# Second mixture's gating inside the second attention by groups of batches, and its two passes with hidden units on partitions

## What is computed

```python
gate_weights = softmax(einsum('bld,de->ble', x, gate_W) + gate_b)      # 8 experts
topk_vals, topk_idx = top_k(gate_weights, 2)
boost = x
for i in range(2):        # experts: relu(x W1[e] + b1[e]) W2[e] + b2[e], hidden 256
    eo = selected_expert(boost, topk_idx[:, :, i], W1, b1, W2, b2)
    outs.append(eo)
    if i < 1: boost = boost + 0.5 * eo
fused = sum(topk_vals[:, :, i:i + 1] * outs[i])
return layer_norm(x + fused, gamma, beta)    # and all of it takes layernorm(x) as its x
```

## Time and profile before

| What | us |
|---|---|
| Median of 3 runs (1680.38 to 1689.57) | 1687.01 |
| The profiled execution | 1688.53 |
| Its span, first to last instruction | 1686.7 |
| Second attention ends | 1390.2 |
| Gating, from there to the first pass's first load | 98.6 |
| First pass | 89.3 |
| Second pass, to the end of the span | 108.6 |

### The profile page before, as it was taken

One profiled execution on the slowest core, in us unless ns is written; L12 is line 12 of the kernel. 1 busy time (PEld: TensorE's weight loads), 2 busy tenths in 40 slices (PEclk: granted clock), 3 DMA queues, 4 the chain that ended last, 5 costly groups with the idle time before them and its releaser, 6 DMA issues. The chain is left out here.

```text
span 1686.7 us, 36701 instructions
## 1 busy us (share of the span) xinstructions
PE 1428.5 (85%) x12500; PEld 940.8 (56%) x12500; DVE 1094.9 (65%) x2690; ACT 858.2 (51%) x1437; POOL 684.8 (41%) x1037
## 2 busy tenths in 40 slices
PE   3799999999999979989999548999999985058583
PEld 1255555555555547669999514555566655046452
DVE  3778778788787726744444447888888745336483
ACT  1567677776766656314444214566666654023242
POOL 2223242332323111463333256566653214635287
PEclk8699999999999989999999867999999995579796
DMA  4111211212112003701212133333332202444341
GB/s 128 57 47 35 64 52 34 66 38 61 51 34 66 20 28 125 101 14 48 49 48 49 30 76 83 76 88 79 78 80 70 72 7 99 144 137 152 88 122 44
DMA packets 92373, 115.54 MB, mean 68 GB/s; under 512 B 13090, under 2 KB 75841, under 8 KB 91936
## 3 DMA queue, kind: packets, MB, share of 16 engines
q1 hardware_dynamic: 75360, 91.63, 19.7%
q0 software_dynamic: 16832, 21.56, 5.6%
HBM read 73.67 MB, written 39.21 MB: 67 GB/s over the span
## 5 line engine op out<-in xcount | busy, mean ns | idle before, releaser
L688 DVE TENSOR_REDUCE wm<-wsm 128x16 f32<-128x512 f32 x512 | 330.1, 685 | 112.7 <-PE wsm L428 109.7
L585 ACT ACTIVATE we<-wst 128x1024 f32<-128x1024 f32 x320 | 325.1, 1022 | 120.0 <-PE wst L461 109.0
L585 ACT ACTIVATE ce<-cst 128x896 f32<-128x896 f32 (+1 forms) x256 | 172.6, 704 | 136.2 <-PE cst L456 116.9
L684 DVE TENSOR_REDUCE cnm<-csm 128x1 f32<-128x512 f32 (+3 forms) x352 | 213.1, 636 | 42.9 <-PE csm L425 37.0
L428 PE MATMUL wsm<-wks,wqs 96*128 96x512 bf16 x512 | 173.4, 394 | 9.1 <-DVE wm L688 5.6
L461 PE MATMUL wst<-wqs,wks 128*128 128x512 bf16 x512 | 149.8, 384 | 0.3 <-ACT we L585 0.3
L1718 PE MATMUL abup<-abxt,abws 128*128 128x128 f32 x1120 | 138.7, 278 | 0.4 <-ACT abxt L1744 0.4
L421 PE MATMUL csm<-cks,cqs 96*128 96x256 bf16 (+3 forms) x512 | 131.5, 309 | 6.9 <-DVE cnm L684 5.0
L1718 PEld LDWEIGHTS abup<-abxt,abws 128*128 128x128 f32 x1120 | 132.6, 194 | 0.7 <-ACT abxt L1744 0.7
L495 PE MATMUL woa<-we,wv 128*32 128x128 f32 (+2 forms) x2560 | 130.6, 340 | 0.0
L814 POOL TENSOR_TENSOR wdif<-wglb,wloc 128x16 f32<-128x16 f32 x32 | 7.1, 221 | 290.2 <-DVE wloc L710 290.2
(11 more groups left out here) (327 smaller groups left out, 3037.1 us busy)
## 6 DMA issues: line engine op xcount, KB each, us to landing
wqs<-qk_parts SPq DMA_DIRECT2D x96, 96.0 KB
wks<-qk_parts SPq DMA_DIRECT2D x96, 96.0 KB
cqs<-qk_parts SPq DMA_DIRECT2D x96, 96.0 KB
cks<-qk_parts SPq DMA_DIRECT2D x96, 96.0 KB
b1r<-rows SPq DMA_DIRECT2D x40, 194.0 KB
qk_parts<-wpt SPq DMA_DIRECT2D x48, 128.0 KB
qk_parts<-cpt SPq DMA_DIRECT2D x48, 128.0 KB
b0r<-rows SPq DMA_DIRECT2D x40, 130.0 KB
```

What stands on the lines that cost most here:

```text
L585: act.activation(E[:, e_slot(g, i), 0:width], ST[:, (U * g + i) % 2, 0:width], ACT.Exp, scale=SCALE).then_inc(s_ex, 1)
L684: dve.tensor_reduce(NM[:, n % 2, first:first + heads, t], got, AX.X, ALU.max).then_inc(s_mx, 1)
L688: dve.tensor_reduce(M[:, n % 2, hs, t, :].rearrange("p (w f) -> p w f", f=DIL), SM[:, j % 2, :].rearrange("p (w i f) -> p w f i", w=NT, f= ...
```

## The change

The second mixture's tiles become an object `Gate` made before the attention. New events in the attention's list gate a finished batch while later batches run: normalise (`g_norm`, `g_rows`), turn and logits (`g_turn`, `g_logits`), and for groups of batches (0,1), (2,3), (4,5), (6), (7) softmax and choice (`g_soft`, four parts), count, places (`g_place`) and scatters. The gated rows lie in a ring of three batches. Running totals of a group (`BASE`) are the next group's bases. After the last slot stand the same events for batch 7, then `finish`: the padding of pass 0 by SP and of pass 1 by ACT, eight blocks each, and the first table; the second table is made by DVE in the first iterations of pass 0. The loads of weights are issued in batches 1, 2 and 7; W2 takes the place of tiles that the attention no longer needs.

In the passes ACT copies the expert's W1 to a fixed tile, which is then the stationary side: the hidden units lie on partitions, b1 is a bias by partition inside the relu, and no transpose of the hidden layer is needed. b2 enters by a product of ones with a tile that has b2 in its first row. All numbers of experts are read at a pass's start; 39 blocks are run. In the second pass ACT takes the root, DVE the reciprocal, the scale and the last addition.

```diff
+        def gating(b, g, at, put):
+            if g == 0 and b in (1, 2, B - 1):
+                put(4, "loads", {1: 0, 2: 1}.get(b, 2))
+            if g == 1:
+                put(3, "g_norm", b - 1)
+                put(6, "g_rows", b - 1)
+            if g == 2:
+                put(1, "g_turn", b - 1)
+                put(3, "g_logits", b - 1)
+            for q, (lo, hi) in enumerate(GROUPS):
+                if b == hi:
+                    if g == 2:
+                        put(4, "g_soft", q, 0)
+                        put(5, "g_soft", q, 1)
+                        put(7, "g_soft", q, 2)
+                    if g == 3:
+                        put(0, "g_soft", q, 3)
+                        put(1, "g_count", q)
+                        put(3, "g_place", q)
+                tiles = [(c, t) for c in range(lo, hi) for t in range(NT)]
+                if b == B - 1 == hi and g == 3:
+                    for c, t in tiles:
+                        put(6, "scatter", c, t)
+                elif b == hi + 1 and hi < B - 1:
+                    for c, t in tiles[2 * g:2 * g + 2]:
+                        put(2 + 3 * (t % 2), "scatter", c, t)
...
         order += [("evac", SLOTS - 1), ("sel", SLOTS - 1), ("heads_T", B - 1), ("out_proj", B - 1)]
+        if gate:
+            b, q = B - 1, len(GROUPS) - 1
+            order += [("g_norm", b), ("g_rows", b), ("g_turn", b), ("g_logits", b)]
+            order += [("g_soft", q, part) for part in range(4)] + [("g_count", q), ("g_place", q)]
+            order += [("scatter", b, t) for t in range(NT)] + [("finish", 0)]
...
+            def g_place(q, turn):
...
+                dve.tensor_copy(PO, counted(T)).then_inc(s_gc, 1)
+                dve.wait_ge(s_gc, q + 1)
+                if q:
+                    for b in range(*GROUPS[q - 1]):
+                        dve.wait_ge(s_sc[b % RING1], 16 * NT * (b // RING1 + 1))
+                bases = [const["base"] if q == 0 else gate.BASE[:, (q - 1) % 2, j, :] for j in range(2)]
+                route.place(st, dve, PO, 0, T, bases)
...
+            for i in range(N + 1):
                 if i + 1 < N:
                     turn_rows(i + 1)
+                if i < N:
...
+                        m = pe.matmul(UP[:, i % 2, c, 0:P], WS[:, i % 2, c * P:(c + 1) * P], XT[:, i % 2, :], start=True,
+                                      stop=True)
...
+                    pe.matmul(Y[:, j % 2, 0:D], const["ones"], B2[:, bass.ds(e * D, D)], start=True, stop=False)
+                    for c in range(HB):
+                        pe.wait_ge(s_h[c], j + 1)
+                        m = pe.matmul(Y[:, j % 2, 0:D], HT[:, j % 2, c, :], W2[:, bass.ds(e * HB * D + c * D, D)],
+                                      start=False, stop=(c == HB - 1))
...
+                    act.copy(WS[:, j % 2, :], W1[:, bass.ds(e * F, F)]).then_inc(s_ws, 1)
...
+                        act.activation(HT[:, i % 2, c, :], UP[:, i % 2, c, 0:P], ACT.Relu, bias=bias(known, i, c)
...
+                    act.activation(std[:, j % K:j % K + 1], mv[:, j % K, 1:2], ACT.Sqrt, bias=eps[:, :]).then_inc(s_sd, 1)
...
+                    dve.tensor_scalar(HT[:, i % 2, 0, :], UP[:, i % 2, 0, 0:P], bias(known, i, 0), 0.0, ALU.add, ALU.max
+                                      ).then_inc(s_h[0], 1)
```

1092 lines of the change are left out of this document (560 added, 532 removed).

## The result

| | kernel before | changed kernel |
|---|---|---|
| median of 20 runs, us | 1685.76 | 1681.22 |
| lowest to highest | 1680.38 to 1689.88 | 1671.97 to 1692.11 |
| ratio | | 0.997 (0.9956 to 0.9985) |
| profiled execution | 1688.53 | 1673.89 |

What follows compares the result with a forecast made beforehand. The prediction took the gating as an uncovered chain and POOL as setting the second pass's end; 1688.53 - 64.6 (gating) + 43 (attention) - 3 - 19 (passes) = 1644.9, forecast 1645 us, range 1612 to 1676.

Steps and rivals of the forecast that it cites:

- The attention's term: Second attention, with the gating moved under it: +43 us, bounded between 15 and 100.
- (a): Slot g1 of the attention: statistics, aggregates, token column and shift on DVE lengthen its windows, 13 us.
- (b): Logits behind `rows` in one bank: PE waits for ACT to empty it, then runs them; 1.9 x 7 = 13 us.
- (c): Groups' softmax, choice, places and counting in the attention, with the last slot's wait for scatters: together 14 us.
- The wait of DVE for scatters in the last slot: Attention's last slot: DVE waits at i3 for scatters POOL issues at i5, PE's last `sel` queued behind; 3.4 us.
- signs of being wrong: In the changed profile: a batch longer by 12 or more, DVE steps of 0.5 and more beside POOL, or ACT busiest in a pass.
- Rival 3: Attention: DVE's small steps stall behind POOL's instructions and stall PE; 1702, deciding from 0.43 us a step; chance 0.1.
- The gating's tail: Gating left after the attention, one batch's, ended by the padding: 34 us in place of 98.6, -64.6.
- The shift: DVE's step in the last batch's gating after the attention: 0.2 us.
- the padding: SP's 8 transfers at 1.56 us in the gating's tail, the later branch, with 2.1 behind to land.
- The passes: Two passes after the gating: 86.0 us (-3) and 89.5 us (-19), at 1.70 us a warm block.
- The sum of cases: Whole kernel: chances added over forecast and rivals, faster by more than about 0.5% 0.90, same 0.03, slower 0.07.

Runs made afterwards that it cites:

- b1_wait7: Kernel before, plus one PE wait behind `rows` in slot g2 of batches 1 to 7, until ACT has emptied the bank; 1683.6 us, ratio 1.003.
- b2_wait28: Kernel before, plus the PE wait behind `rows` in all 28 slots whose rows belong to batches 1 to 7; 1703.2 us, ratio 1.0142.
- c_after: The changed kernel without an edit, run again on chip 2; 1634.8 us, ratio 0.9755 to the kernel before.
- d1_fixed: Changed kernel, PE in the passes always taking expert 0's W2 and b2 and reading no table; 1678.6 us, ratio 0.994 to the kernel before.
- a2_lazy: Changed kernel, each engine in the passes reading a table word when first needed, not ten ahead; 1640.5 us, ratio 0.9776 to the kernel before.

## Why the prediction was wrong

**The attention's term failed, +43 for +70.8.** By its parts:
- (a), slot g1, forecast 13: the seven windows grew by 20.9, by 3.0 in batches 1, 2 and 4 and by 5.0 in batch 3. In batch 3 POOL's scatters for the first group fall into the same slot, beside its gathers for the first mixture; that this makes the 5.0 is not tested (batch 5 has scatters too, and grew by 3.3). In batch 1 DVE's work is 2.0 more than in the earlier trace rows (12.35 for 10.40), about as forecast, but its idle time grew by 1.0 too, and PE waited 1.0 for score maxima behind the burst.
- (b), the wait for the bank, 1.9 a batch: right where the clock held (1.8 in batch 3). The stall's own price is shown by b1_wait7 and b2_wait28, 0.7 to 0.9.
- (c), the groups, and (b) together: slots g2 and g3 were to grow by 30 (POOL's 3 among them) and grew by 48.3. In it are 22 for the clock, and without them 26. Within this, what I had not seen is that PE itself would stand at the count, 8.4 us in three places; I had priced the steps on DVE and forgotten who waits for their end. The wait of DVE for scatters in the last slot was 6.4, not 3.4, by the view of its waits:

```profile
DVE bAT L1371 <- DMA rows<-brows,bIDX: 6.4, 1, 6.4
```

- The step that failed is one that the working doesn't have. I read "granted 0.53" in the earlier trace rows as a property of the gating, and 1.00 in every window of the earlier trace rows as a given. PE's own products were priced at full clock, and waits at their length. That a stage at full clock can lose it when waits of 1 to 3 us are put in it was neither a term nor a rival; it is worth some 22 of the 28 us missing. The other 6 to 8 are waits of PE beyond those priced: idle time grew by 36, and 28 were forecast for it. c_after bears this out: with 27.2 us at half clock its attention is 61.9 longer than that of the kernel before (364.7 for 302.8), and less half of 27.2 this is 48, as 70.8 less 22 is 49. What exactly makes the clock fall at one place and not at its twin isn't settled by these runs.

Of the signs of being wrong that were named, one was met: a batch longer by 12 or more. The three windows of batches 2 and 4 grew by 12.4 each, where 8 was forecast, those of batches 1 and 3 by 8.1 and 6.9, where 4 was.

**Rival 3 fell, though the time lies in its range.** It was to come about by DVE steps of 0.43 us and up; the 1681 came about another way. DVE's routing steps in the attention beside POOL's work, the window of their line alone (busy time, count, then clock and DMA):

```profile
1085.00:1459.00 374.00, 30.41 (x129) 0.94 0.27 72
```

and one of the groups of that line (count, shortest, median and longest in ns):

```profile
L1371 DVE TENSOR_TENSOR bV<-bV,cgmx x8: 191/225/1054, 1159.7 to 1438.4; 128x64 f32<-128x64 f32 x6, 128x32 f32<-128x32 f32 x2
```

30.41 us in all, 0.236 each; four of the 129 took 1.05 to 1.12 beside an instruction of POOL (the 1054 above is one). The rule of the Trainium skill ("SBUF — State Buffer", section "SBUF: two separate sides") thus shows at single steps, and at the shift of the last batch, but does not decide the time.

**The gating's tail was right.** 35.9 for 34. The shift took 1.23 beside POOL's addition where I had taken 0.2, and the padding ended it, as forecast. Its two last parts were off in opposite ways: the padding took 10.2 for 12.5, and 6.9 passed from its end to the first load (1494.95) where 2.1 were taken. The timeline of the changed kernel:

```profile
1461.80 1.25 POOL L1129 TENSOR_TENSOR brows<-X,bbe 128x512 f32<-128x512 f32 x1
...
1461.85 1.23 DVE L624 SCALAR_TENSOR_TENSOR cgsh<-cgmv,cgrs 128x4 f32<-128x4 f32 x1 [1.36 <-POOL cgrs L1121]
...
1477.91 10.16 SPq L1205 DMA_DIRECT2D rows<-bze  x8
```

**The passes were right in number, by luck.** 87.4 and 89.9 for 86.0 and 89.5. But PE's block is 1.23, not 1.56: the starts of products in the earlier trace rows lie apart by more than the products need. The first transpose came 5.8 after the load, not 2.6. In the first pass the start was 3.2 over, the blocks 2.9 under (65.5 for 68.4) and the end 1.1 over. And 1.70 a block, taken as "some late starts stay" from the 1.82 of the kernel before, met 1.72 and 1.77 only because of the standstills. The kernel before has its share of the two levels: 1.64 a block in its first pass with b1_wait7's edit on chip 4, 1.81 in the profile that I read; no stretch of half a microsecond without PE, ACT and DVE is in that pass, so whether it is the same thing isn't shown. Where the blocks are short the changed kernel takes 33 us less in the passes, and at 1634.8 would have been inside the range; that too would have been luck, since the attention's term was 19 short there and the passes' 31 too long. What was forecast as one number has two.

**The chances.** The sum of cases put 0.9 on a gain of over 0.5 %; the gain was 0.3 %. Every case took full clock for the attention, so they shared one error and the range was too narrow above.

## To carry to other kernels

Where PE is busy without a break at full clock, a wait put in its path costs about its length and at times 1.7 to 3.4 us more, the half of a stretch of 3.4 or 6.8 at half clock; look for the granted clock of every window, not only for the idle time. A small product that needs a bank emptied, or the end of a chain on another engine, goes a unit or more behind that point: two numbers changed in the order gave 14 to 19 us here. And measure the kernel before and the changed one on more than one chip before a ratio is believed: the same two programs stood at 0.9755 and at 0.9988.

## What the runs showed of the hardware

- Run on several chips, the same program differs by 45 to 50 us (1634.8, 1680.0, 1685.2), the kernel before by 6 to 9. Of this some 33 lie in the two passes, where on the slower level about every third or fourth block takes 2.5 to 4.5 us in place of 1.23; in most such places of the first pass PE, ACT and DVE stand still together for 0.5 to 1.3 us. Another 9 to 16 lie in the attention, together with 17 to 24 us more at half clock.
- 28 waits of 0.7 to 1.2 us in a stream that has none above 0.4 before did not make the granted clock fall once (b2_wait28), while the changed kernel, with 21 idle stretches of 0.9 us or more, had six, seven, nine and nine falls of 3.4 or 6.8 us in four executions. Each began in such a stretch or at most 2.4 us behind one.
- Ten reads of a table word in a row on PE put a pass's first transpose 3.7 us later (5.8 us after the first load in the changed kernel, 2.2 in d1_fixed and a2_lazy); spread over the blocks they cost as much (1.41 for 1.31 us a block in the first pass).
